# A conditioned transformer block on one core: w_mod loaded first, two scores ahead of the second projection, another order of the last batch

## What is computed

```python
mod = jax.nn.swish(c) @ w_mod + b_mod
sh_msa, sc_msa, g_msa, sh_mlp, sc_mlp, g_mlp = jnp.split(mod, 6, axis=1)
xn = _ln(x) * (1 + sc_msa[:, None, :]) + sh_msa[:, None, :]
qkv = xn @ w_qkv + b_qkv                      # then q, k, v by heads
q = _ln(q, g_q); k = _ln(k, g_k)
attn = jax.nn.softmax(jnp.einsum('bhqd,bhkd->bhqk', q, k) * HD ** (-0.5), axis=-1)
o = (attn @ v) @ w_proj + b_proj
x = x + g_msa[:, None, :] * o
xn2 = _ln(x) * (1 + sc_mlp[:, None, :]) + sh_mlp[:, None, :]
h = jax.nn.gelu(xn2 @ w1 + b1, approximate=True)
x = x + g_mlp[:, None, :] * (h @ w2 + b2)
```

## Time and profile before

| | us |
|---|---|
| median of 3 runs | 204.37 (201.6 to 204.68) |
| the profiled execution | 202.29 |
| its span, first to last instruction | 200.5 |

### The profile page before, as it was taken

One profiled execution on the slowest core, in us unless ns is written; L12 is line 12 of the kernel. 1 busy time (PEld: TensorE's weight loads), 2 busy tenths in 40 slices (PEclk: granted clock), 3 DMA queues, 4 the chain that ended last, 5 costly groups with the idle time before them and its releaser, 6 DMA issues.

```text
span 200.5 us, 3873 instructions
## 1 busy us (share of the span) xinstructions
PE 166.0 (83%) x1504; PEld 93.9 (47%) x1504; DVE 125.7 (63%) x312; ACT 108.9 (54%) x146; POOL 65.5 (33%) x81
## 2 busy tenths in 40 slices
PE   0009982749979999999999999899659999999983
PEld 0005131413434454544644545344316796979773
DVE  3269568819548587679677774955856786564212
ACT  2001024255998879978888799976842404132320
POOL 8103513067418146173290201600462352220000
PEclk9999999999999999999999999999856999999999
DMA  0993028950000000000000000000000000101101
GB/s 10 247 211 120 5 51 251 399 158 0 3 2 0 3 3 0 0 3 0 3 0 5 0 3 2 0 3 0 3 0 0 0 3 0 60 3 59 59 0 59
DMA packets 4535, 8.67 MB, mean 43 GB/s; under 512 B 821, under 2 KB 3071, under 8 KB 4406
## 3 DMA queue, kind: packets, MB, share of 16 engines
q1 hardware_dynamic: 4228, 8.41, 14.0%
q10 hardware_dynamic: 288, 0.01, 0.1%
HBM read 7.21 MB, written 1.21 MB: 42 GB/s over the span
## 4 chain that ended last, share of the span: by engine, by line
PE 73%; DVE 9%; DMA 6%; ACT 3%; POOL 3%; issue 3%; SPq 1%; POOLq 0%; ACTq 0%
PE ps_o L1103 15%; PE ps_o L1226 10%; PE ps_s L1209 9%; PE ps_s L1088 8%; PE ps_x L1022 8%; DMA pTs<-in_b_mod 6%; PE ps_x L1029 4%; PE ps_o L1131 4%; PE ps_x L1113 4%; PE ps_s L1006 3%; PE ps_o L1015 3%; PE ps_x L1197 2%; PE ps_s L1000 2%; POOL z2s L464 2%; DVE kst L753 2%
## 5 line engine op out<-in xcount | busy, mean ns | idle before, releaser
L552 ACT ACTIVATE pTs<-ps_s,escale 128x1024 f32<-128x1024 f32 x64 | 68.9, 1109 | 17.1 <-PE ps_s L1088 16.1
L1103 PE MATMUL ps_o<-pTs,v 128*32 128x256 f32 x512 | 42.9, 410 | 5.0 <-ACT raw L523 2.5
L609 ACT ACTIVATE late<-ps_s 120x512 f32<-120x512 f32 (+1 forms) x20 | 11.9, 596 | 26.1 <-PE ps_s L1209 26.1
L1088 PE MATMUL ps_s<-qT,kT 32*128 32x256 f16 x256 | 24.3, 282 | 1.0 <-DVE qT L777 1.0
L1226 PE MATMUL ps_o<-w_sb,late 120*128 120x144 f32 (+1 forms) x160 | 20.7, 287 | 0.7 <-ACT late L609 0.7
L1226 PEld LDWEIGHTS ps_o<-w_sb,late 120*128 120x128 f32 (+1 forms) x160 | 19.9, 190 | 1.2 <-ACT late L609 1.2
L1209 PE MATMUL ps_s<-late,w1s 110*120 110x512 f16 (+1 forms) x80 | 18.8, 386 | 0.0
L1103 PEld LDWEIGHTS ps_o<-pTs,v 128*32 128x32 f32 x512 | 10.5, 110 | 17.5 <-ACT pTs L552 7.1
L1088 PEld LDWEIGHTS ps_s<-qT,kT 32*128 32x128 f16 x256 | 7.1, 93 | 24.4 <-issue 20.8
L464 POOL TENSOR_TENSOR z2s<-z2s,mbc 128x576 f32<-128x576 f32 x4 | 8.4, 2092 | 28.7 <-DVE z2s L901 28.7
L397 POOL COPY v<-raw 128x288 f32<-128x288 f32 x8 | 4.0, 496 | 41.8 <-DVE ssum L726 34.9
(11 more groups left out here) (115 smaller groups left out, 263.4 us busy)
## 6 DMA issues: line engine op xcount, KB each, us to landing
mbc<-mod_rows SPq DMA_DIRECT2D x6, 432.0 KB, 7.4
late<-in_w SPq DMA_DIRECT2D x1, 990.0 KB
xall<-in_x SPq DMA_DIRECT2D x1, 864.0 KB, 13.6
out<-late SPq DMA_DIRECT2D x3, 288.0 KB, 2.3
z2s<-in_w_qkv SPq DMA_DIRECT2D x1, 742.5 KB
mbc<-mod_rows SPq DMA_DIRECT2D x2, 288.0 KB, 6.4
pTs<-in_w_mod SPq DMA_DIRECT2D x1, 486.0 KB
w_sb<-in_w SPq DMA_DIRECT2D x1, 337.5 KB
```

The source lines that it names most:

```text
L552: nc.scalar.activation(pT[u % NP].rearrange("p g n -> p (g n)"), ps_s[:, 2 * (u % 2):2 * (u % 2) + 2, :].rearrange("p a n -> p (a n)"), AC ...
L609: nc.scalar.activation(hT[k % 2][0:FW[f], f, :], ps_s[0:FW[f], (NF * k + f) % 4, :], ACT.Gelu_apprx_tanh, scale=UNSCALE).then_inc(gelued, 1)
L1088: mm = nc.tensor.matmul(ps_s[:, 2 * (u % 2) + a, half * N:(half + 1) * N], kT[par][rows, j, i * P:(i + 1) * P], qT[par][rows, j, :], start ...
L1103: mm = nc.tensor.matmul(ps_o[SLOT * g:SLOT * (g + 1), 1, (j % 2) * N:(j % 2 + 1) * N], v[par][:, i, h, :], pT[u % NP][:, g, :], start=(i = ...
```

## The change

The diff does five things. (1) SyncE issues w_mod and b_mod first, then w_qkv and lo_row, then x of batches 0 and 1, and waits for that x before it issues the rest. (2) VectorE does gain and flag first, then the weights' mean, then x's statistics, then the centring, and standardises and scales batch 0 ahead of the low half of w_qkv; ScalarE takes the roots of x after the copies of scale and shift. (3) `scores(0, 1)` stands ahead of `make_qkv(1)`. (4) w1 is split early: GpSimd's half after `iteration(1, 1)`, VectorE's in two halves at the end of iterations 3 and 4. (5) The last batch: statistics in two parts (8 tiles in iteration 6, then 4), pair 0 standardised in iteration 6, z transposed in halves through another bank between the units, and pair 1's hidden layer begun inside pair 0's. Core of the diff, engine by engine:

SyncE:

```diff
             xp = x.rearrange("b (p i) c -> p b (i c)", i=I)
-            sp.dma_start(xall[:, 0:2], xp[:, 0:2]).then_inc(ld_x, 16)
+            sp.dma_start(wm_sb[0:HT], w_mod).then_inc(ld_wm, 16)
+            sp.dma_start(wm_sb[HT:HT + 1, 0, :], b_mod.rearrange("(o c) -> o c", o=1)).then_inc(ld_wm, 16)
             sp.dma_start(wq_f, w_qkv).then_inc(ld_wq, 16)
             sp.dma_start(lo_row[:], lo_rows).then_inc(ld_wq, 16)
...
+            sp.dma_start(xall[:, 0:2], xp[:, 0:2]).then_inc(ld_x, 16)
             sp.dma_start(id32[:], ident).then_inc(ld_id, 16)
+            sp.wait_ge(ld_x, 16)
             sp.dma_start(xall[:, 2:B], xp[:, 2:B]).then_inc(ld_rest, 16)
```

GpSimd:

```diff
             iteration(0, 0)
             iteration(1, 1)
+            pool.wait_ge(ld_w1, 16)
+            nc.gpsimd.tensor_scalar(w1_h, w1_f, WS, lo_row[:, 0:1], ALU.mult, ALU.mult).then_inc(w1_made, 1)
             for it in range(1, 2):
```

ScalarE (READY is 8 tiles, EARLY 12; `x_roots(first_stats)` moves behind the two copies of scale and shift, L501 and L502):

```diff
+            def early_roots(part, r):
+                act.wait_ge(stat2, r.stop)
...
                 exponentials(n, 3)
-                if not makes:
-                    early_roots()
+                if n == B - 2:
+                    early_roots(0, slice(0, READY))
                 exponentials(n, 4)
...
                 exponentials(n, 6)
+                if not makes:
+                    early_roots(1, slice(READY, EARLY))
                 exponentials(n, 7)
...
-            output(B - 1, 1, 1)
...
+                    if (k, f) == (0, 2):
+                        output(B - 1, 1, 1)
```

VectorE, first the opening, behind the gain and the flag:

```diff
+            dve.wait_ge(ld_wq, 32)
...
+            nc.vector.tensor_reduce(wq_m[:], wh, AX.X, ALU.add).then_inc(D.sem, 1)
+            dve.wait_ge(ld_x, 16)
+            x_stats(first_stats)
+            x_aggregate(first_stats)
+            done("mean")
+            nc.vector.scalar_tensor_tensor(wh, wq_m[:].unsqueeze(3).broadcast_to([KR, NC, 2 * NH, HD]), -1.0 / HD, wh,
+                                           ALU.mult, ALU.add).then_inc(D.sem, 1)
+            x_newton(first_stats)
             dve.wait_ge(ld_id, 16)
             nc.vector.tensor_copy(id16[:], id32[:]).then_inc(D.sem, 1)
...
+                nc.vector.tensor_scalar(xt[:, i, :], xi[:, i, :], mv[:, i, 0:1], rstd[:, i:i + 1],
+                                        ALU.subtract, ALU.mult).then_inc(prep.mx.sem, 1)
...
+            nc.vector.tensor_tensor(xt[:], xt[:], mb(0, A1), ALU.mult).then_inc(prep.mx.sem, 1)
...
-            standardise_first()
-            modulate_first()
+            shift_first()
             stack(0, prep)
```

VectorE, the iterations and the last batch (`split_weights`, L701, stays ahead of `shift_first`):

```diff
+            def roots(part, tiles):
+                if part < 2:
+                    dve.wait_ge(root_act.sem, root_act.after(part, "y0"))
...
+            def first_half_z():
+
+                roots(0, ready)
+                standardise2(0)
+
+            def w1_half(c):
+
+                dve.wait_ge(w1_made, 1)
+                nc.vector.scalar_tensor_tensor(w1s[:, c:c + 2], w1_f[:, c:c + 2], WS, w1_h[:, c:c + 2],
+                                               ALU.mult, ALU.subtract).then_inc(w1_made, 1)
...
+                if n == B - 2:
+                    aggregate(ready)
...
+                if n == B - 2:
+                    first_half_z()
                 if n >= 2:
                     residual(n - 2)
+                if n in (3, 4):
+                    w1_half(2 * (n - 3))
...
             projected(B - 3)
             normalise(B - 2)
+            stack2(0)
             residual(B - 3)
+            channels(B - 2)
+            zT_half(0, 0)
+            standardise2(1)
+            zT_half(0, 1)
+            dve.wait_ge(w1_made, 3)
+            nc.vector.memset(hT[1][FW[-1]:FW[-1] + 1, NF - 1, :], 1.0).then_inc(h_ones, 1)
+            projected(B - 2)
             aggregate(early)
...
+            stack2(1)
+            roots(1, early)
             residual(B - 2)
+            zT_half(1, 0)
+            zT_half(1, 1)
+            standardise2(2)
             normalise(B - 1)
...
             channels(B - 1)
+            stack2(2)
             projected(B - 1)
             residual(B - 1)
...
+            roots(2, late_tiles)
+            standardise2(3)
             final(0)
```

TensorE (the bank of z's transposes is x's, `x_bank`, for pairs 0 and 1):

```diff
             scores(0, 0, 0)
+            scores(0, 1, 0)
             make_qkv(1, prep)
...
+            def transpose_z_half(k, h):
+                pe.wait_ge(ln2_parts.sem, ln2_parts.after(k, "zlo"))
+                if k < 2 and (k or h):
+                    pe.wait_ge(ln2_T.sem, ln2_T.after(k, f"zT{h}") - 1)
...
-            values(n, 0, par)
             scores(n, 2, par)
             transpose_o(n - 1, 1 - par)
+            values(n, 0, par)
             values(n, 1, par)
...
             scores(n, 5, par)
+            pe.wait_ge(gated, n - 1)
+            transpose_z_half(0, 0)
             values(n, 4, par)
             scores(n, 6, par)
             project(n - 1)
             values(n, 5, par)
             scores(n, 7, par)
+            transpose_z_half(0, 1)
             values(n, 6, par)
+            pe.wait_ge(w1_made, 3)
+            hidden(0, range(0, 2))
+            values(n, 7, par)
+            pe.wait_ge(exped, B * U)
+            hidden(0, range(2, 4))
+            transpose_z_half(1, 0)
+            hidden(0, range(4, NF))
             pe.wait_ge(gated, B - 1)
...
             transpose_o(n, par)
+            transpose_z_half(1, 1)
+            hidden(1, range(0, 2))
             transpose_o_tok(n)
...
             pe.wait_ge(o_out, B * 2)
             mlp_out(0, range(0, 1))
+            project(n)
+            mlp_out(0, range(1, 2))
+            hidden(1, range(2, NF))
             pe.wait_ge(gated, B)
...
+            transpose_z(2)
+            mlp_out(1)
+            for k in range(2, NB):
```

More of the change, by code:

```diff
@@ L858, in residual, with standardise2 @@
                     nc.vector.bn_stats(bst[:, n * I + i, :], xall[:, n, i * H:(i + 1) * H]).then_inc(res_dve.sem, 1)
+            def standardise2(k):
+                if k:
+                    dve.wait_ge(ln2_mod.sem, ln2_mod.after(k - 1, "za"))
+                xk = xall[:, 2 * k:2 * k + 2, :].rearrange("p b (i c) -> p (b i) c", i=I)
+                for t in range(T):
+                    nc.vector.tensor_scalar(z2[:, t, :], xk[:, t, :], mv2[:, T * k + t, 0:1],
+                                            rstd2[:, T * k + t:T * k + t + 1],
+                                            ALU.subtract, ALU.mult).then_inc(ln2_z.sem, 1)
@@ new lines, in stack2 @@
+            def stack2(k):
+                dve.wait_ge(ln2_mod.sem, ln2_mod.after(k, "zm"))
+                if k:
+                    dve.wait_ge(ln2_pe.sem, ln2_pe.after(k - 1, "zT1"))
+                zc = z2m.rearrange("p t (c w) -> p (t c) w", w=CW)
+                slots = zst[:, :, 0:3 * CW].rearrange("p t (s w) -> p t s w", w=CW)
+                nc.vector.tensor_copy(slots[:, :, 0:3:2, :], zc.unsqueeze(2).broadcast_to([P, T * NC, 2, CW])
+                                      ).then_inc(ln2_parts.sem, 1)
+                dve.wait_ge(ln2_parts.sem, ln2_parts.after(k, "zhi"))
+                nc.vector.tensor_tensor(slots[:, :, 1, :], zc, slots[:, :, 0, :], ALU.subtract).then_inc(ln2_parts.sem, 1)
@@ new lines, in zT_half, with zT_out, aggregate @@
+            def zT_half(k, h):
+                dve.wait_ge(ln2_pe.sem, ln2_pe.after(k, f"zT{h}"))
+                if k >= 2:
+                    dve.wait_ge(hid_pe, NF * (k - 1))
+                nc.vector.tensor_copy(zT[k % 2][:, 2 * h:2 * h + 2, :], z_bank(k, h)[0:KR]).then_inc(ln2_T.sem, 1)
+            def zT_out(k):
+                for h in range(2):
+                    zT_half(k, h)
+            def aggregate(tiles):
+                dve.wait_ge(res_dve.sem, res_dve.after((tiles.stop - 1) // I, "bn1"))
+                for t in tiles:
+                    nc.vector.bn_aggr(mv2[:, t, :], bst[:, t, :]).then_inc(stat2, 1)
@@ new lines, in roots @@
+            def roots(part, tiles):
+                if part < 2:
+                    dve.wait_ge(root_act.sem, root_act.after(part, "y0"))
+                dve.wait_ge(stat2, tiles.stop)
+                r = slice(tiles.start, tiles.stop)
+                newton(nc, dve, root_dve, part, nt2[:, r], y2[:, r], mv2[:, r, 1], rstd2[:, r])
+                dve.wait_ge(root_dve.sem, root_dve.after(part, "rstd"))
+            ready, early, late_tiles = range(READY), range(READY, EARLY), range(EARLY, B * I)
```

133 lines of the change are left out of this document (28 added, 105 removed).

## The result

| | before | changed |
|---|---|---|
| median | 203.38 us (4 runs, 201.6 to 204.68) | 194.37 us (4 runs, 192.2 to 195.04) |
| profiled execution, its span | 202.29, 200.5 | 193.88, 192.1 |

The ratio is 0.957, with a 95% interval of 0.944 to 0.970: faster by 9.0 us in the medians, by 8.4 us in the two spans. Forecast was 6.7 less than the profiled 202.3, and 196.6 us for the median. Executions of one and the same kernel differ by up to 2.3% on one chip; the ratios here compare the fast executions of each kernel on one chip, the medians take all of them.

The account below looks back on a forecast made before the run. TensorE, busy 83% of the span, was taken as the bound, losing time to opening loads, last-batch waits and a lower clock. Gains 0 + 0.9 + 0.9 + 4.9 = 6.7 off 202.3 gave 195.6; named 196.6 us, range 191.5 to 202.

Parts of the forecast that it names:

- Opening: Loads and batch 0's preparation: w_mod's 5.4 us goes into a wait for VectorE; gain 0, bounds -0.7 to +4.6.
- Rival A: Opening gains too, as loads land sooner or VectorE is not held: about 3 us more, 192.6; chance 0.17.
- the landings: Opening loads, reordered at their old pace: w_mod lands at 9.7, w_qkv at 13.6, x at 15.1 us.
- the bounds: Limits on the opening's gain, -0.7 to +4.6 us; fewer bytes in flight would make its chain 3.0 shorter.
- a Newton step held as said: Opening: VectorE's second Newton step is held beside GpSimd's conversion, ending at 19.7 us and lasting over 1 us.
- Second score: Batch 0: both scores first puts exponential 1 under the projection; gain 0.9 us, bounds 0.4 and 1.1.
- w1's split: Iteration 6: without GpSimd's 2.38 us there, VectorE's split of k is no longer held 1.73 us; gain 0.9.
- Last batch: Last batch and MLP: 4.1 us idle removed, 3.95 from the clock staying up, less 3.2 of new waits; gain 4.9.
- The wait ahead of values 7: Last batch: TensorE idles 1.35 us because exponential 7 stands behind the second early roots and VectorE's aggregate.
- rival B: Last batch: the clock falls once more around the 1.35 us wait, costing 3.95 us, 199.6; chance 0.25.
- C: Last batch: the clock falls and stays down, with TensorE idle over 2 us; 203.5 with two low stretches; chance 0.05.
- D: Last batch is ScalarE's and waits only move: 1.8 from the middle terms, at most 1 from the end, 200; chance 0.08.

Follow-up runs that it names:

- queue_only: Kernel before with only the load order changed (w_mod, b_mod, then w_qkv, lo_row, then x), no hold of the rest: ratio 1.010 (1.005 to 1.014).
- after_xfirst: Changed kernel with x of batches 0 and 1 back at the head of the queue, the hold kept: ratio 0.971 (0.965 to 0.977) of before.
- scores_only: Kernel before with only scores(0, 1) moved ahead of make_qkv(1): ratio 1.000 (0.995 to 1.004).
- w1_only: Kernel before with only w1's split moved as in the change, last batch's order as before: 199.51 us beside 204.0 for before.

## Why the prediction was right or wrong

- **Time and direction** were right: 194.37 us lies in the range, 2.2 under the number named. Part of that is luck: of the 8.4 us between the two profiles, the opening brought 3.24 where the sum had 0, and batch 0 lost 1.74 (2.76 in the second profile) that the sum did not have, so that two errors partly cancel. The last stretch, 5.8 forecast and measured, was added up from parts of another size.
- **Opening, 0 forecast, 3.24 measured.** Rival A, at 0.17, is what happened, though mostly by an earlier start of the bytes and less by the hold it was argued from. The step that failed is the landings: "w_mod 8.53 - 1.5 + 2.7 = 9.7, w_qkv 13.6, x 15.1". They were 7.3, 11.5 and 12.1. Order alone moves the first to 7.39 (queue_only), x back at the head moves it to 10.59 (after_xfirst), and the hold, to which the bounds gave up to 3.0 us (bytes in flight), is 0.8. The rest of that chain was nearly right: statistics to transposes forecast 25.1 - 15.1 = 10.0 us, measured 21.90 - 12.80 = 9.10, with a Newton step held as said; some steps of that chain overlap where I added them end to end.
- **Second score, 0.9 forecast.** The mechanism and the size to the first values were right (1.10 and 1.12). The weak step is the tacit one, that what the first values gain the end gains: the stretch behind them depends on when TensorE's clock rises (8.58 to 13.12 us), and that was in no term. How much of the 0.9 reaches the end on average is open; scores_only (1.000, 0.995 to 1.004) excludes neither all of it nor nothing.
- **w1's split, 0.9 forecast, 4.5 measured alone.** The gain up to the last batch is right (0.8 by the sixth output projection). The size is off since I booked GpSimd's faster modulation, and with it the clock, under the order of the last batch.
- **Last batch, 4.9 forecast, 1.3 measured on top of w1.** Together 5.8, as forecast, in one profile each. The wait ahead of values 7 was placed rightly and sized 1.35 for 1.04; the 0.85 ahead of pair 1 is 0.79. The clock stayed up (rival B did not come, nor C, nor D). But its fall in before is not simply the child of the wait of 1.73 us: w1_only has the same wait, the same busy time ahead of it, and no fall. And rival B's lower bound, gaps of up to 0.9 us that left the clock alone, was read too low: before has a wait of 1.20 us at 58.42, behind ScalarE's oT, with no fall after it. What decides the fall is open.
- **Rival A** deserved more than its 0.17: the trace of before has almost no bytes before 4 us, though x was issued at 1.2. I read the landings and not the start.

## What to carry to other kernels

Look at when the first bytes of an opening move, not only at the order of landings: here the transfer at the head of the queue set the start of all others. A gain ahead of the point where TensorE's clock rises may not reach the end; cut the profiles behind that point, and compare the two pieces by themselves. A profile is of one execution: before it explains a ratio, look where that execution's time lies among the others. When a long conversion moves, price what ran beside it in its old place on both engines: here that was the larger part of the gain.

## What the runs showed of the hardware

- The rise of TensorE's clock for good came between 39.6 and 55.4 us in kernels whose transposes start between 21.78 and 25.98 us, and at 49.5 and 51.2 in two profiles of one kernel. Between the extremes the same stretch of work takes 8.58 and 13.12 us. The Trainium skill's TensorE: Matmul & The Clock Gate (The HAM clock gate) says that the transition from the lower to the higher level varies from run to run, by 0.5 us either way. The trace agrees that it varies, but by more: the two profiles of one kernel are 1.7 us apart. The same section of the Trainium skill says that the monitor behind it is not reset when a kernel starts, which no run here can show. Why the new order of batch 0 has more of the late rises (four of the eight profiles with the scores ahead and no added matmuls later than 51 us, none of the four without) is open.
- A load of 288 KB in 256 rows at the head of SyncE's queue let 2 GB/s move in the stretch from 2 to 4 us, one of 486 KB in 72 rows 106, and the first in two halves 54.
- GpSimd's conversion from 32 to 16 bits held VectorE's two-input step (1.55 instead of 0.16 us), a cast from SBUF (1.07 instead of 0.45) and a standardising (2.01 instead of 0.61), and left copies from PSUM alone (0.69 and 0.68, with it and without). In the other direction, GpSimd's modulation took 4.15 us in before, where VectorE's split of w1 (2.54 us) runs beside it, and 1.42 without that.
